# Attention row-sum reciprocals: four block transposes replaced by one transpose and a trip through device memory

## The reference

```python
x = x + attn(layernorm(x))            # 16 heads of 32, rotary, causal, softmax(q k^T / sqrt(32)) v, @ Wo.T
x = x + xattn(layernorm(x), ctx)      # 32 heads of 16, axial rotary, softmax(q k^T / 4) v, @ Wout + bout
x = x + ffn(layernorm(x))             # silu(gate) * up, then down; integer weights minus 128, scaled; hidden 1408
```

## Time and profile before

| | |
|---|---|
| median of 3 runs | 1691.74 us (1691.45 to 1694.11) |
| the profiled execution: its own time | 1692.19 us |
| its span, first to last instruction | 1690.4 us |
| mean granted TensorE clock | 0.994 of 2.4 GHz |
| attention phase, feed-forward phase | up to about 1175 us, and from there |
| one loop turn | 35.17 us, 27 of them |
| busy: PE, DVE, ACT, POOL | 97%, 68%, 58%, 33% |

### The profile page before, as it was taken

One profiled execution on the slowest core, in us unless ns is written; L12 is line 12 of the kernel. 1 busy time (PEld: TensorE's weight loads), 2 busy tenths in 40 slices (PEclk: granted clock), 3 DMA queues, 4 the chain that ended last, 5 costly groups with the idle time before them and its releaser, 6 DMA issues. The chain is left out here.

```text
span 1690.4 us, 40585 instructions
## 1 busy us (share of the span) xinstructions
PE 1644.9 (97%) x14608; PEld 1287.1 (76%) x14608; DVE 1150.1 (68%) x2087; ACT 972.1 (58%) x3817; POOL 552.5 (33%) x535
## 2 busy tenths in 40 slices
PE   6899999999999999999999999988999999999997
PEld 4677777777777777777777777766888888888885
DVE  7777778877788777887778877786744344344332
ACT  6577777777777776777767777675522222222221
POOL 4444444444444444444444444441011011011011
PEclk9999999999999999999999999998999999999999
DMA  6011111011110011111110011021520120120110
GB/s 213 29 32 31 36 48 36 30 30 36 48 35 30 30 36 51 32 30 31 35 53 30 30 34 35 23 70 51 187 75 9 66 74 14 61 74 19 56 50 26
DMA packets 55097, 80.98 MB, mean 48 GB/s; under 512 B 4880, under 2 KB 25488, under 8 KB 55056
## 3 DMA queue, kind: packets, MB, share of 16 engines
q1 hardware_dynamic: 55056, 80.43, 14.6%
HBM read 63.63 MB, written 16.78 MB: 48 GB/s over the span
## 5 line engine op out<-in xcount | busy, mean ns | idle before, releaser
L877 ACT ACTIVATE prob<-bank,nmax 128x128 f32<-128x128 f32 x1536 | 541.4, 408 | 153.4 <-DVE nmax L1099 147.6
L877 ACT ACTIVATION_READ_ACCUMULATOR prob<-bank,nmax 128x1 f32 x1536 | 381.0, 248 | 0.0
L1099 DVE TENSOR_REDUCE nmax<-bank 128x4 f32<-128x512 f32 x376 | 233.4, 682 | 71.0 <-PE bank L536 70.3
L1504 PE MATMUL fbank<-shared,piece_hi 128*128 128x512 f32 x1152 | 280.3, 394 | 0.0
L1504 PEld LDWEIGHTS fbank<-shared,piece_hi 128*128 128x128 f32 x1152 | 215.8, 187 | 53.2
L399 POOL TENSOR_TENSOR rope_buf<-rope_buf 128x512 f32<-128x512 f32 x128 | 168.1, 1324 | 175.0 <-DVE rope_buf L1052 174.9
L1656 DVE SCALAR_TENSOR_TENSOR h<-fbank,su_c,sil 128x512 f32<-128x512 f32 x88 | 65.9, 749 | 198.6 <-PE fbank L1504 197.1
L449 POOL TENSOR_TENSOR cn_l<-cn,cn_h 128x512 fp32r<-128x512 f32 x64 | 83.0, 1296 | 240.0 <-DVE cn L1091 240.0
L1590 ACT ACTIVATE sil<-fbank,sg_c 128x512 f32<-128x512 f32 x88 | 60.6, 688 | 173.2 <-PE fbank L1504 172.1
L1596 ACT ACTIVATE h_h<-h 128x512 fp32r<-128x512 f32 x88 | 55.6, 632 | 175.0 <-DVE h L1656 175.0
L512 PE MATMUL bank<-shared,z1T_h 128*128 128x512 f32 x520 | 140.4, 412 | 4.2 <-ACT shared L860 2.6
(11 more groups left out here) (171 smaller groups left out, 3130.0 us busy)
## 6 DMA issues: line engine op xcount, KB each, us to landing
xA<-in_x SPq DMA_DIRECT2D x32, 256.0 KB, 2.9
xB<-in_x SPq DMA_DIRECT2D x32, 256.0 KB, 2.8
x_scratch<-x SPq DMA_DIRECT2D x32, 256.0 KB, 2.0
shared_loaded<-x_scratch SPq DMA_DIRECT2D x8, 1024.0 KB, 7.7
xr<-x_scratch SPq DMA_DIRECT2D x8, 1024.0 KB, 5.6
out<-xr SPq DMA_DIRECT2D x8, 1024.0 KB, 4.3
cx<-in_ctx SPq DMA_DIRECT2D x32, 128.0 KB, 2.3
range_window<-in_wg SPq DMA_DIRECT2D x27, 112.0 KB, 2.0
```

Of the source, the lines that this page charges most:

```text
L877: last = nc.scalar.activation(prob[:, c, i, :], S[c][:, i * P:(i + 1) * P], ACT.Exp, bias=nmax[:, c, i:i + 1], accum_out=rs[:, h:h + 1])
L1099: nc.vector.tensor_reduce(out=nmax[:, c, :], in_=S[c][:, :].rearrange("p (g k) -> p g k", g=G), op=ALU.max, axis=AX, negate=True).then_inc ...
L1504: last = nc.tensor.matmul(dst[:, :], w[:, k, cols], z[:, k, :], start=(n == 0), stop=(n == len(passes) * KT - 1))
```

## The change

In all turns but the last few sequences, the four block transposes go. TensorE transposes `rinv1` (or `rinv2`) itself, once, into 16 (or 32) rows of the bank `PA`, straight behind the transposes of the probabilities. ScalarE copies these rows to `rows1` or `rows2`. SyncE stores them to device memory, waits for the store, and loads them back in 4 (or 8) DMAs, each of which spreads 512 numbers over 32 (or 16) partitions of `rT1` (or `rT2`). To make the 512 numbers lie in one stretch, the row sums are kept in another order of columns (`sums_column`). GpSimd's `spread` is left only in `last()`, for `rinv1` of the last sequence and `rinv2` of the last two, in the old form. Some semaphores are merged: the three of the feed-forward weight pieces are one now, and ScalarE waits for all three pieces ahead of the first.

```diff
+            def broadcast_rows(n, q, stored):
+                rows, dram, dst = ((rows1, rows1_dram, rT1), (rows2, rows2_dram, rT2))[n - 1]
+                blocks = G * n
+                sp.wait_ge(rw_r[n], q + 1)
+                sp.dma_start(dram[:, :], rows[:, :]).then_inc(rw_out, 16)
+                sp.wait_ge(rw_out, 16 * stored)
+                for b in range(blocks):
+                    sp.dma_start(dst[P // blocks * b:P // blocks * (b + 1), :],
+                                 dram[KT * b:KT * (b + 1), :].rearrange("j t -> (j t)").partition_broadcast(P // blocks))\
+                        .then_inc(rT_in[n], 16)
+
             def turn(sq, cq, nx, nz, oq):
+                if oq is not None:
+                    broadcast_rows(2, oq, oq + sq + 1)
                 if sq is not None and cq is not None and not isinstance(sq, int):
                     sp.wait_ge(rng_r, cq - 1)
...
                 if oq is not None:
                     sp.wait_ge(x2_r, oq + 1)
                     sp.dma_start(x2_dram[oq, :, :], x2[:, :]).then_inc(x2_out, 16)
+                if sq is not None:
+                    broadcast_rows(1, sq, sq + 1 if oq is None else oq + sq + 2)
...
-                    pe.wait_ge(rb_r[2], oq + 1)
-                    if has_c:
-                        pe.wait_ge(zT_hi[2], cq + 1)
-                        pe.wait_ge(zT_lo[2], cq + 1)
-                    transpose4(TC, columns(rbc2[:, :, :].rearrange("p h d -> p (h d)"))).then_inc(ri_d[2], 1)
...
                 if has_s:
                     transpose_prob("1", sq)
+                    pe.wait_ge(ri_r[1], sq + 1)
+                    if has_c:
+                        pe.wait_ge(rT_r["q2"], cq + 1)
+                    nc.tensor.transpose((PA if has_c else TC)[0:H1, 0:P], rinv1[:, :], ident[:, :]).then_inc(ri_d[1], 1)
...
-                    transpose4(TC, columns(rbc1[:, :, :].rearrange("p h d -> p (h d)"))).then_inc(ri_d[1], 1)
                 if has_n and has_c:
+                    pe.wait_ge(rw_r[1], sq + 1)
                     project_q1(nx)
...
                 if has_c:
                     transpose_prob("2b", cq)
+                    pe.wait_ge(ri_r[2], cq + 1)
+                    if has_n:
+                        pe.wait_ge(rT_r["k1"], nx + 1)
+                    nc.tensor.transpose(PA[0:H2, 0:P], rinv2[:, :], ident[:, :]).then_inc(ri_d[2], 1)
...
+            def copy_rows(n, q, src):
+                act.wait_ge(ri_d[n], q + 1)
+                rows = (rows1, rows2)[n - 1]
+                nc.scalar.activation(rows[:, :], src[0:H1 * n, 0:P], ACT.Copy).then_inc(rw_r[n], 1)
...
             def context1(q):
-                dve.wait_ge(riT_r[1], q + 1)
+                if isinstance(q, int) and q == L:
+                    dve.wait_ge(riT_r[1], 1)
+                else:
+                    dve.wait_ge(rT_in[1], 16 * G * (q + 1))
                 dve.wait_ge(av_d[1], q + 1)
                 normalise_ctx(1, PC, rT1)
...
                 if has_c:
+                    row_sums2(cq)
                     even_copies("2b", cq)
-                if has_c:
-                    row_sums2(cq)
```

More of the change, by code:

```diff
@@ L403, in spread @@
                 wait(pool, ri_d[n], q)
+                if n == 2:
+                    pool.wait_ge(ri_d[1], B)
                 pool.wait_ge(ri_r[n], q + 1)
-                pool.tensor_tensor(tile[:, :, :], r[:, :].unsqueeze(2).to_broadcast([P, h, w]),
-                                   one_c[:, :].unsqueeze(2).to_broadcast([P, h, w]), ALU.mult).then_inc(rb_r[n], 1)
+                blocks = h // KT
+                for j in range(KT):
+                    last = pool.tensor_tensor(tile[:, blocks * j:blocks * (j + 1), :],
+                                              r[:, :].rearrange("p (b j) -> p b j", j=KT)[:, :, j:j + 1].to_broadcast([P, blocks, w]),
+                                              one_c[:, :].unsqueeze(2).to_broadcast([P, blocks, w]), ALU.mult)
+                last.then_inc(rb_r, 1)
             def split_ctx(q):
@@ L457, in turn @@
                     rope_sum("q1", nx)
-                    spread(1, sq, rinv1, rbc1, H1, DK1)
                     rope_sum("k2", sq)
@@ L484, in turn @@
                     key_pairs(sq)
-                if cq is not None:
-                    spread(2, cq, rinv2, rbc2, H2, DK2)
             rough_rstd(1, 0)
@@ L963, in turn @@
                 if has_c:
-                    exponentials("2a", cq, (1, 2, 3))
+                    exponentials("2a", cq)
                     odd_copies("2a", cq)
@@ L1112, in row_sums @@
                 dve.wait_ge(p_r[1], G * (q + 1))
[L1113 removed]
+                wait(dve, ri_d[1], q)
                 nc.vector.reciprocal(rinv1[:, :], rsum1[:, :]).then_inc(ri_r[1], 1)
@@ L1117, in row_sums2 @@
                 dve.wait_ge(p_r[2], 2 * G * (q + 1))
-                wait(dve, rb_r[2], q)
+                if isinstance(q, int) and q == L:
+                    dve.wait_ge(rb_r, 2)
+                else:
+                    wait(dve, ri_d[2], q)
                 nc.vector.reciprocal(rinv2[:, :], rsum2[:, :]).then_inc(ri_r[2], 1)
             def context1(q):
-                dve.wait_ge(riT_r[1], q + 1)
+                if isinstance(q, int) and q == L:
+                    dve.wait_ge(riT_r[1], 1)
+                else:
+                    dve.wait_ge(rT_in[1], 16 * G * (q + 1))
                 dve.wait_ge(av_d[1], q + 1)
@@ L1126, in context2 @@
             def context2(q, src):
-                dve.wait_ge(riT_r[2], q + 1)
+                if isinstance(q, int) and q >= M:
+                    dve.wait_ge(riT_r[2], q - M + 1)
+                else:
+                    dve.wait_ge(rT_in[2], 32 * G * (q + 1))
                 dve.wait_ge(av_d[2], 2 * q + 2)
```

77 lines of the change are left out of this document (39 added, 38 removed).

## The result

The changed kernel takes 1802.1 us (median of 4 runs, 1796.6 to 1810.0) where the kernel before takes 1691.6 (median of 4): the ratio is 1.065, with a 95% interval of 1.063 to 1.068. The forecast was 1842 us and slower. The direction and the mechanism hold, and the sizes do not: the cost of a turn was put at 5.0 us and is 2.5 to 4.9 in the loop, 3.2 on average. That is a third less, and the forecast was 40 us too high.

A forecast was written before the change was run, and what follows sets the result against it. The prediction took TensorE, busy 97% of the span, to bound the kernel. It charged 5.0 us for each of 30 turns, 150 us on a span of 1690.4, and with small corrections forecast 1842 us, range 1795 to 1910.

The forecast's parts named there:

- The store, 2.0 and 0.16: In each trip on SyncE: the store of the rows lands after 2.0 us, the first load is issued 0.16 later.
- Eight issues 0.43 apart: On SyncE, in rinv2's trip: the eight loads of rT2 are issued one every 0.43 us.
- Landing 2.0: At the end of each trip: the last load of the rows lands 2.0 us after its issue.
- Together: rinv2's whole trip, from row copy to VectorE: context2, and o2 behind it, start 2.6 us later.
- `xA` 3.8 late: xA's load, queued on SyncE behind rinv2's nine DMAs: VectorE's statistics of xA come 3.8 us later.
- `v2` 4.45 late: On TensorE: v2 starts 4.45 us later, behind a 1.7 us wait to transpose rinv1.
- The second trip ends 0.55 us behind `v2`'s delay: rinv1's trip, ahead of context1: context1 and o1 start 5.0 us later, with v2's 4.45 contained in it.
- The low sum: Lower bound with landings of 1.7 and issues every 0.39: second trip adds nothing, some 3.8 us a turn, 1806 us.
- The turn keeps its shape: Behind o1, up to the probabilities' transposes at the turn's end: nothing new is late.
- That the clock falls in each turn: Rival: TensorE's clock falls in the new pause ahead of o2, 1.5 us a turn, 1887 us; chance 0.18.
- The sign: Whole kernel: slower 0.94, faster 0.05, same 0.01; rinv2's trip had 4.8 us from copied rows to today's context2.
- the rival that forecast a gain: Rival: both trips hidden, rT2 landing in time for context2; 0.5 us a turn saved, 1677 us; chance 0.04.

The follow-up runs named there:

- x_floor: Changed kernel, loop contexts multiplied by an unchanging tile (no division by row sums), rinv2's trip behind xA's load, first attention's reciprocals ahead of normalise 1; 1693.5 us.
- x_no_wait: Changed kernel, loop contexts multiplied by an unchanging tile (no division by row sums), VectorE waiting for the row loads only later in the turn; 1817.5 us.
- x_double: Changed kernel with sixteen loads of 8 partitions for rT2 instead of eight of 16, same bytes; 1861.2 us.
- x_xa_first: Changed kernel with SyncE issuing the loads of the windows, cx, xB and xA ahead of rinv2's trip; 1771.7 us.
- x_best_two: Changed kernel with rinv2's trip behind xA's load, first attention's reciprocals ahead of normalise 1, and rT2 loaded by two 128 KB DMAs instead of eight; 1766.0 us.

## Why the prediction was right, and where its sizes were not

**The steps, against the turn at 751.54.** Counted from the row copy of `rinv2` as in the prediction:

- *The store, 2.0 and 0.16.* From its issue (750.63) to the first load (752.02) pass 1.39 us, not 2.16. I had taken the landing of a 256 KB store for one of 16 KB and reasoned that size doesn't matter. It does: 1.4 against 2.0. That is the main mis-sized term, once in each trip. The price that I weighed by the Trainium skill (DMA: Bandwidth & Descriptors, Anatomy of one DMA: device memory is the heaviest target of the last write) is farther still from these rows: the stores land ahead of the small loads, 1.4 against 1.8 and 2.0. That section describes DMAs that GpSimd issues, and these are SyncE's, so the rows tell only that its ranking can't be carried over to them.
- *Eight issues 0.43 apart.* Right: 3.56 us for eight, and `xA` 2.76 us behind the first window (I had 2.63).
- *Landing 2.0.* 1.8 and 2.0. Right.
- *Together*, `context2` starts 6.76 us after the row copy began; by my numbers it would have been 7.7. Before it started 5.1 us after that point, so it is 1.7 us late, not 2.6.
- *`xA` 3.8 late.* It is 3.07 by the same measure (10.99 us behind the row copy's start; before 7.92). The store's 0.77 again.
- *`v2` 4.45 late.* It is 3.09 (14.37 against 11.28). TensorE's wait for `rinv1` was put at 1.7 and is 1.64. But I moved VectorE's whole stretch from `xA` to `rinv1` with its pause: before, `add_cross` waits 0.51 us for `o2` in it, and when all of it comes late that pause is gone (3.07 us in place of 3.51).
- *The second trip ends 0.55 us behind `v2`'s delay.* It adds nothing, or 0.1 us as in this turn. The comparison itself was sound, since `context1` was taken to move with `v2` and only the 0.55 beyond it was charged. The size was not: the second trip's store is 0.77 us faster too, and 0.55 less 0.77 leaves nothing. VectorE's four maxima of 2.48 us hang on TensorE and come as late as it does, and the last load (issued at 767.98) lands as they end. The low sum, with a store of 1.7, had found the same.
- *"The turn keeps its shape" behind `o1`.* It does: 14.73 us to the transposes of the probabilities, 14.78 before. Behind these stand two small pauses of TensorE, 0.22 us inside the transposes of `z` and 0.39 us ahead of `scores1`, which make `scores1` 0.45 us later. They don't lengthen this turn, since TensorE waits 1.76 us ahead of `o2` and 1.64 ahead of the transpose of `rinv1` afterwards, for things that hang on SyncE. `x_floor` has them too, without such waits, and its turn is still the shortest of all. What a bank costs that a small transpose borrows, no run here shows by itself.

So 5.0 us is 2.8 on average at full clock (37.93 less 35.17), which over 25 turns makes 69 of the loop's 80 us.

**The clock.** That the clock falls in each turn was a rival with a chance of 0.18. It falls in 6 of 25 turns and costs 1.8 us each, 11 us of the 112; the rival's price was 1.5. The reason that spoke against it, pauses shorter than the one of 2.96 us in the earlier trace rows, is what the runs show: with pauses of 1.8 and 1.6 us a turn the clock mostly holds, with one of about 3 us it fell in 24 of the 25 turns of `x_no_wait` and in 19 of those of `x_double`. In `x_xa_first`, whose pauses are 1.3 to 1.7 us on the rows of PE but for one of 3.0, it fell in the turn with that one alone. By the Trainium skill (TensorE: Matmul & The Clock Gate, The HAM clock gate) idleness brings the throttled state back; the traces agree, for the longer pauses, and they don't bear out that each turn's pause does it.

**What the sum had too cheap.** I gave every place with both trips the price of a loop turn, and up to 1.5 us to the first two. The first four turns lose 19 us instead of about 13, and the last trip and what stands behind it in the queue lose 8 us instead of 5 (the two turns between, like the loop, lose less than they were charged, 5 us instead of 10). In the first four the clock is 0.89 to 0.96, against 0.94 to 1.00 in the kernel before; several of the trips are slower at both places (last section); and the load of the second phase's first tiles stands behind the last trip, which I hadn't looked for in `last()`. These terms, about 9 us, hide a part of the loop's error, and that is luck.

**The sign.** It hung on one comparison: 4.8 us between the copied rows and today's `context2`, against a round trip with eight issues that no row let me put under 6.5. It takes 6.5 (750.60 to 757.11), and the experiments add the other half: even with both trips free the turn gains 0.27 us, half of what I had allowed the rival that forecast a gain (1.24 less 0.7). TensorE's saved transposes stand ahead of projections that wait for VectorE's products anyway, which is why the prediction counted them at nothing.

## What to carry to other kernels

Before a store with loads that wait for it goes into a queue, list what stands behind it in every turn and behind the loop: its latency is paid where its result is used, its issues by all that follows, and loads that could go already belong ahead of it. Ask of the work that a change saves what its successor waits for; TensorE was busy 97% of the time, and the two blocks of 0.42 us that it no longer did in a turn bought 0.27, since the next projection's input came from VectorE nearly as late as before. When one wait is taken away the next late arrival takes its place, sometimes as one longer pause that costs more than the two before.

## What the runs showed of the hardware that I had not expected

- Stores of 8 and 16 KB from 16 and 32 partitions to device memory land after 1.4 us, a dependent load is issued 1.39 us after the store's issue; stores of 256 KB land after 2.0.
- SyncE issues loads that write 8 partitions every 0.34 us, those that write 16 every 0.45.
- The same 256 KB of repeated rows take 1.8 us to landing from the last of eight loads (5 us from the first issue), 3.9 us from the issue of one load with an outermost dimension of eight, and 5.2 us from the first of two with four each (583.21 to 588.43 in `x_best_two`).
- Where SyncE passes a piece of its program for the first time, trips are often slow. In the changed kernel these are nine: the seven in the turns outside the loop, and the two of the loop's first turn (135.90 and 152.61), which are the loop's own instructions, so that constant addresses are not the reason. In five of the nine the first load is issued 2.1 to 3.1 us after the store and not 1.4 (70.03 to 72.63, 1212.19 to 1215.15), and in three of the four with eight loads these take 4.63 to 4.76 us to issue and not 3.56 (the earlier trace rows had 0.50 as the longest interval; this is 0.6). From the second turn of the loop on all is as fast as elsewhere.
- What coincides with it are DMA packets of 16 KB on another queue, of the kind "instruction". The DMA view of the changed kernel has them in its third part, for 152 to 156 us and for 1212 to 1220, the last trip:

```profile
q8 instruction: 1, 0.02, 1.5%
```

```profile
q8 instruction: 2, 0.03, 1.6%
```

  From 190 to 196 us, with the same trip one turn later, it has none. In the 13 kernels with trips, 59 of the 63 intervals from store to first load that exceed 1.6 us have such a packet in them, and 13 of the other 670. So loading of the program is the likely cause; the packets don't name the engine whose program it is, and no run kept everything else and took them away.
- Not settled is why the second turn of `x_floor` lasts 37.1 us, at a clock of 0.95, where nothing of a trip is waited for.
